# Attention on one core: TensorE's instruction order planned over all sixteen passes at once, row maxima turned six units into the next pass, outputs copied out of PSUM one or two tiles later

## The reference

```python
scores = jnp.einsum('bhqd,bhkd->bhqk', q, k) * scale
causal = jnp.tril(jnp.ones((t, t), dtype=bool))
scores = jnp.where(causal[None, None], scores, -jnp.inf)
att = jax.nn.softmax(scores, axis=-1)
y = jnp.einsum('bhqk,bhkd->bhqd', att, v)
```

## Time and profile before

| what | us |
|---|---|
| median of three runs (lowest 3022.57, highest 3024.21) | 3024.12 |
| the profiled execution, its own time | 3017.77 |
| its span, first to last instruction | 3015.9 |
| attention: the maxima of pass 0 alone | 366.9 to 467.4 |
| attention: first scores to the last copy | 467.4 to 2120.4 |
| busy over the span: PE, DVE, ACT, POOL | 2606.6, 1957.8, 1479.5, 775.3 |

### The profile page before, as it was taken

The page is one execution under the profiler, slowest core; times in us unless marked ns, Lnnn a source line. Parts: engine busy times, 40 slices in busy tenths (PEclk is TensorE's granted clock), DMA queues, the critical chain, the costliest instruction groups (busy, mean ns, idle before and its releaser), DMA issues. The chain is left out here.

```text
span 3015.9 us, 46437 instructions
## 1 busy us (share of the span) xinstructions
PE 2606.6 (86%) x16224; PEld 1332.4 (44%) x16225; DVE 1957.8 (65%) x2820; ACT 1479.5 (49%) x2726; POOL 775.3 (26%) x836
## 2 busy tenths in 40 slices
PE   6988189999999999989999999998666689898880
PEld 6545023333333333333333333332455577787770
DVE  4666297778777877867877787770364333465564
ACT  0555105777767777757777777778222211111110
POOL 0344401111110111011011001111348322474554
PEclk7989558999999999999999999999877799999995
DMA  3577871414531551452355134000764422453443
GB/s 109 143 217 206 161 97 57 100 46 100 117 67 58 121 109 53 81 117 68 57 117 103 36 59 69 13 9 16 200 189 161 152 89 90 126 164 117 133 135 121
DMA packets 210668, 315.39 MB, mean 105 GB/s; under 512 B 31312, under 2 KB 154336, under 8 KB 208192
## 3 DMA queue, kind: packets, MB, share of 16 engines
q1 hardware_dynamic: 163984, 206.55, 29.6%
q0 software_dynamic: 28944, 90.60, 10.1%
q10 hardware_dynamic: 17568, 16.00, 1.5%
HBM read 159.05 MB, written 153.22 MB: 104 GB/s over the span
## 5 line engine op out<-in xcount | busy, mean ns | idle before, releaser
L967 DVE TENSOR_REDUCE mxc<-ps 128x2 f32<-128x1024 f32 (+4 forms) x1168 | 1292.4, 1149 | 297.7 <-PE ps L859 148.5
L949 ACT ACTIVATE probs<-ps 128x512 f32<-128x512 f32 (+1 forms) x2240 | 1159.4, 589 | 400.9 <-PE ps L885 387.3
L859 PE MATMUL ps<-ks,qs 96*128 96x512 bf16 (+3 forms) x2560 | 701.4, 364 | 89.7 <-DMA vs<-v_ones 67.1
L885 PE MATMUL ps<-qs,ks 99*128 99x512 bf16 (+3 forms) x2560 | 686.9, 349 | 10.2 <-ACT probs L949 8.1
L899 PE MATMUL ps<-probs,vs 128*32 128x512 f32 (+3 forms) x5120 | 596.6, 543 | 13.2 <-POOL probs L822 13.2
L859 PEld LDWEIGHTS ps<-ks,qs 96*128 96x128 bf16 x2560 | 205.2, 99 | 554.4 <-issue 202.4
L822 POOL TENSOR_SCALAR_AFFINE_SELECT probs<-probs 128x512 f32<-128x512 f32 x256 | 162.9, 647 | 960.2 <-ACT probs L949 959.0
L885 PEld LDWEIGHTS ps<-qs,ks 99*128 99x128 bf16 x2560 | 221.3, 97 | 421.9 <-ACT probs L949 301.7
L1527 ACT ACTIVATE hid_t<-ps 128x512 f32<-128x512 f32 x125 | 74.7, 597 | 495.2 <-PE ps L1500 451.6
L1500 PE MATMUL ps<-x_t,w_at 128*128 128x128 f32 x2000 | 264.7, 288 | 48.4 <-DVE w_at L1548 41.6
L1500 PEld LDWEIGHTS ps<-x_t,w_at 128*128 128x128 f32 x2000 | 244.2, 199 | 90.3 <-issue 64.9
(11 more groups left out here) (171 smaller groups left out, 1910.4 us busy)
## 6 DMA issues: line engine op xcount, KB each, us to landing
ks<-k_parts SPq DMA_DIRECT2D x96, 256.0 KB, 15.3
qs<-q_parts SPq DMA_DIRECT2D x96, 256.0 KB, 16.2
v_ones<-vout SPq DMA_DIRECT2D x64, 256.0 KB, 4.5
vs<-v_ones SPq DMA_DIRECT2D x16, 1024.0 KB, 26.0
attn_t<-o_sb SPq DMA_DIRECT2D x64, 256.0 KB, 4.7
xs<-slot_x SPq DMA_DIRECT2D x128, 128.0 KB
slot_y<-ys ACTq DMA_DIRECT2D x122, 128.0 KB, 1.7
slot_x<-zero POOLq DMA_DIRECT2D x24, 640.0 KB, 6.2
```

The costliest lines, as they stand in the source:

```text
L859: ins = pe.matmul(o[:, h, :], qs[0:SROWS, r, h0 + h, i * P:(i + 1) * P], ks[0:SROWS, r, h0 + h, 512 * c:512 * c + w], start=first, stop=no ...
L885: ins = pe.matmul(o[:, h, :], ks[0:SROWS + MROWS, r, h0 + h, j * P:(j + 1) * P], qs[0:SROWS + MROWS, r, h0 + h, J * QJ + lo:(J + 1) * QJ], ...
L949: act.activation(probs[:, (NKT * r + m) % NPB, h0:h0 + nh, 0:QJ - lo], st_view(r, s), ACT.Exp, scale=DH ** -0.5).then_inc(exp_done, 1)
L967: dve.tensor_reduce(mxc[:, h0:h0 + nh, i, c], red_view(u, g0), AX_X, ALU.max).then_inc(red_done, 1)
```

## The change

The list is made once for all 16 passes by a new class `Course`, with other costs, with a model of GpSimd's masks and split, of VectorE, and of the landing of the maxima's rows. It chooses among the instructions that its model holds ready by which of ScalarE and VectorE would run dry first. How far VectorE's units may run ahead of the scores is a share of a pass (`RUN_AHEAD`). The turn of pass n stands after unit 5 of pass n+1 on all engines (`LATER`), also at the start, where ten units stood behind the turn. ScalarE copies a block out after the exps of the second tile that follows it (`OUT_LAG`), also over the border of two passes. TensorE waits for the maxima's rows at the first scores of each pass and for a pass's loads at its unit 0. GpSimd's and SP's code is unchanged. The diff, cut to its core:

```diff
--- before.py
+++ after.py
@@ -585,58 +585,129 @@
-def plan(tiles, sets, of_tile, last, diag, groups, nst, npb, cut, turn_at, qj):
-
-    MM, EXP, RED, MASK, COPY, CROSS, BACK, SWITCH = 1 / 2400, 0.81e-3, 1.04e-3, 0.834, 0.58, 0.2, 0.13, 0.14
...
-        if g < len(groups):
-            free = red_end[-2] + BACK if g > 1 else 0.0
-            if (g < near and share[g] <= (done[s - 1] if s else 0) / done[start[cut] - 1] + 0.01) or (
-                    g >= near and s >= start[turn_at]):
-                now.append((free, "group", g))
...
-        at, kind, x = next((c for c in now if c[0] <= pe + 0.1), None) or min(now)
...
+class Course:
+
+
+    MM, MUL, MASK, ENTER, LEAVE, LATE, HOP = 1 / 2400, 0.0045, 0.0565, 0.09, 0.147, 0.1, 0.2
+    TURN_PE, TURN_DVE, ROWS, SPLIT, AFFINE, OUT, LAST_MAX, LOAD = 0.29, 0.5, 3.0, 1.6, 0.65, 0.58, 0.45, 30.0
+    RUN_AHEAD, PREFER_DVE = 0.16, 0.3
...
+        while s < ns * nit or v < nv * nit or g < len(self.stream):
...
+                n, u = self.stream[g]
+                at = red_end[g - self.nred] + hop if g >= self.nred else 0.0
+                if u == turn_unit:
+                    ok = n in parts
+                    at = max(at, parts.get(n, 0.0) + hop)
+                else:
+                    ok = g <= first_turn or s >= ns * nit or dve_at[g] <= (
+                        1 + s // ns + share[s % ns] + self.RUN_AHEAD) * per_group
+                if u == 0 and n >= 3:
+                    ok = ok and n in loaded
+                    at = max(at, loaded.get(n, 0.0))
+                if ok:
+                    now.append((at, "unit", n, u))
+            if s < ns * nit:
+                n, x = divmod(s, ns)
+                tile = n * nv + sets[x][0]
+                before = tile - self.out_lag - 1
+                ok = n in rows_in and v > tile - self.npb and not (before >= 0 and before % nv in self.last and v <= before)
+                if ok and not (n + 1 < nit and x == self.of_tile[self.first_masked][-1] and n + 1 not in neg):
+                    at = exp_end[s - self.nst] + hop if s >= self.nst else 0.0
+                    now.append((max(at, rows_in[n]) if x == 0 else at, "scores", n, x))
...
+                if v in ready and (j > 0 or out < 0 or out in out_end):
+                    now.append((max(ready[v], out_end[out] if j == 0 and out >= 0 else 0.0) + hop, "values", n, m))
+            base = pe + (self.LEAVE if kind == "values" else 0.0)
+            urge = {"unit": dve - pe, "scores": act - pe - self.PREFER_DVE, "values": 1e9}
+            free = [c for c in now if c[0] <= base]
+            at, what, n, x = min(free, key=lambda c: urge[c[1]]) if free else min(now)
...
+                if h0 == 0:
+                    before = tile - self.out_lag - 1
+                    if before >= 0 and before % nv in self.last:
+                        act = max(act, values_end[before] + hop) + self.OUT
+                        out_end[before // nv * self.nj + tiles[before % nv][0]] = act
+                    if tile >= self.npb:
+                        act = max(act, values_end[tile - self.npb] + hop)
+                act = max(act, pe + hop) + self.exp(nh * w)
+                exp_end.append(act)
...
+                    if m in self.diag:
+                        pool = max(pool, act + hop) + self.AFFINE
+                        ready[tile] = pool
...
-        AHEAD = 10
-        NRING = NGRP + 1
-        CUT, TURN_AT = 34, 37
-        entry_of = [(1, u) for u in range(AHEAD, NGRP)] + [(1, TURN)] + [(2, u) for u in range(AHEAD)]
...
+        LATER = 6
+        OUT_LAG = 2
+        NRED = 2
+        assert NSET * R % NST == 0 and NKT * R % NPB == 0
+
+        STREAM = []
+        for n in range(NIT):
+            STREAM += [(n, u) for u in range(LATER)] + [(n - 1, TURN)] * (n > 0) + [(n, u) for u in range(LATER, NGRP)]
+        STREAM.append((NIT - 1, TURN))
+        unit_at = {x: at for at, x in enumerate(STREAM)}
+        ORDER = Course(KT, SETS, of_tile, LAST, DIAG, [GROUPS[u][3:] + (GROUPS[u][1] == GROUPS[u][0] // 4,) for u in range(NGRP)],
+                       STREAM, NST, NPB, NRED, OUT_LAG, QJ, DIAG[-KPJ]).order(NIT)
...
-        RECIP_AT = 30
+        RECIP_AT = 40
...
-                def group(r, u, at, g0):
+                def group(n, u, at):
-                    diag = c == i // 4
-                    if not isinstance(at, int) or at >= 2:
-                        pe.wait_ge(red_done, at - 1)
+                    r, o, diag = n % R, red_view(u, at), c == i // 4
+                    if u == 0:
+                        pe.wait_ge(ld[r], LD * (n // R + 1))
+                    if at >= NRED:
+                        pe.wait_ge(red_done, at - NRED + 1)
...
+                    if s == 0:
+                        pe.wait_ge(m_ld, M_LD * n + M_LD + 1)
                     pe.wait_ge(exp_done, NSET * n + s + 1)
...
-                def entry(n, r, q):
-
-                    ahead, u = entry_of[q]
-                    at = NRING * n + RING0 + q
-                    if u == TURN:
-                        turn(n + 1, at, q)
+                pe.wait_ge(pool_init, R)
+                for kind, n, x in ORDER:
+                    if kind == "scores":
+                        scores(n, n % R, x)
+                    elif kind == "values":
+                        values(n, n % R, x)
+                    elif x == TURN:
+                        turn(n, unit_at[n, x])
                     else:
-                        group((r + ahead) % R, u, at, q)
-
-                def body(n, r, i, more=True, far_more=True):
-                    pe.wait_ge(m_ld, M_LD * n + M_LD + 1)
-                    for kind, x in ORDER:
-                        if kind == "scores":
-                            scores(n, r, x)
-                        elif kind == "values":
-                            values(n, r, x)
-                        elif more and (far_more or entry_of[x][0] == 1):
-                            if entry_of[x] == (2, 0):
-                                pe.wait_ge(ld[(r + 2) % R], LD * i + LD * ((r + 2) // R + 1))
-                            entry(n, r, x)
-
-                pe.wait_ge(ld[0], LD)
-                for u in range(NGRP):
-                    group(0, u, u, u)
-                pe.wait_ge(ld[1], LD)
-                turn(0, NGRP, NGRP)
-                for u in range(AHEAD):
-                    group(1, u, NRING + u, u)
-                pe.wait_ge(pool_init, R)
-                for n in range(NIT):
-                    body(n, n % R, n // R, n + 1 < NIT, n + 2 < NIT)
+                        group(n, x, unit_at[n, x])
...
-                        if m - 1 in LAST.values():
-                            output(n, KT[m - 1][0])
-                    output(n, NJ - 1)
-
-                for n in range(NIT):
-                    body(n, n % R)
+                def exps(n, r, m):
+                    lo = KT[m][2]
+                    act.wait_ge(pv_done, NKT * n + m + 1)
...
+                for tile in range(NIT * NKT + OUT_LAG + 1):
+                    n, m = divmod(tile - OUT_LAG - 1, NKT)
+                    if n >= 0 and m in LAST.values():
+                        output(n, KT[m][0])
+                    if tile < NIT * NKT:
+                        exps(tile // NKT, tile // NKT % R, tile % NKT)
...
-                def body(n, far_more=True):
-                    for q, (ahead, u) in entries(far_more):
-                        if q == RECIP_AT and n > 0:
-                            reciprocals(n - 1)
-                        at = NRING * n + RING0 + q
-                        if u == TURN:
-                            turn(n + 1, at, q)
-                        else:
-                            group(u, at, q)
-                            if u == NGRP - 1:
-                                maxima(n + 1, at + 1)
-
-                for u in range(NGRP):
-                    group(u, u, u)
-                maxima(0, NGRP)
-                turn(0, NGRP, NGRP)
-                for u in range(AHEAD):
-                    group(u, NRING + u, u)
-                for n in range(NIT - 1):
-                    body(n, n + 2 < NIT)
+                for at, (n, u) in enumerate(STREAM):
+                    if u == RECIP_AT and n > 1:
+                        reciprocals(n - 2)
+                    if u == TURN:
+                        turn(n, at)
+                    else:
+                        group(u, at)
+                        if u == NGRP - 1:
+                            maxima(n, at + 1)
```

156 lines of the change are left out of this document (86 added, 70 removed).

## The result

The changed kernel takes 3059.70 us (median of four runs, 3053.58 to 3061.55); the kernel before, run beside it, 3024.16 (3022.57 to 3030.34). The ratio is 1.0115, with a 95% interval of 1.0100 to 1.0131: 35.5 us slower, where 21 us less were forecast. The profiled execution took 3060.03 us, with a span of 3058.1. Of all executions in this document one, of the kernel with the turn at once further down, ran at a granted clock of 0.80, where that kernel's others have 0.92, and took 3415.92 us; it counts in that kernel's median and not in its ratio.

The account below looks back on a forecast made before the run. TensorE bounds a pass, busy 102.63 of 103.54 us. Start 2.0, borders 16.8, passes 4 and 8 -1.0, last pass 3.5 sum to 21.3 off 3017.8; plus 6.3 for the median gives 3002.8 us, range 2991 to 3018.

Parts of the forecast that it names:

- The denominators' wait: Nine passes with fills: VectorE wants the denominators' read earlier, TensorE waits 0 to 2.2 us in each; 0.3 taken.
- each us by which they start later behind the fills is paid back in part: Loads after the block 3 copy: started later they take less time, 30.6 us without fills instead of 37.7.
- my latest bound: Denominators' read in passes with fills: lands at most 2.9 us later, at 716.6, a TensorE wait of 2.2.
- The fixed capacity shared by two streams: DMA engines, loads beside fills: if they only shared capacity, the end of both would not move; wait 0.
- My rival with the full wait: Read lands 2.9 later in nine passes, TensorE waits 2.2 in each: 3021 us; chance 0.17 for about halfway or more.
- the likeliest range of 2996 to 3010: Whole kernel, median time: the forecast case's own range around 3002.8 us, chance 0.55.
- The start: Before the first scores: they come at about 464.8 instead of 467.42; gain 2.0 us, bounds 0 and 3.
- Passes 4 and 8: GpSimd's stuck fill stays: pass 4 loses 2 us, pass 8 gains 1; net loss 1, between loss 4 and gain 5.
- The floor of a pass, and the border: Border of two passes, 14 times: waiting there goes, a pass lasts 101.9 to 102.0 us, a gain of 1.6.
- the slower rival that I priced: Block copies, later by four exps, hold the next block's values at 60 places: 3030 to 3039 us; chance 0.05.
- The last pass: Last pass, with the end of pass 14: 3.5 of 5.4 us gained, bounds 0 and 5.4; full tiles stay at 2.46.
- my 1.6: Gain in us forecast for each border of two passes, before 0.2 off for small waits.

Follow-up runs that it names:

- the kernel with the turn at once: Changed kernel with the turn right behind its maxima (`LATER = 0` instead of 6) and fills behind the mask of tile 23: 3011.90 us, ratio 0.9960.

## Why the prediction was wrong

It failed at one term, and by a smaller sum at another. Both are landings of transfers.

**The denominators' wait: the failed step.** The prediction named the mechanism, and the profile after has it word for word. What failed is "I expect the read 0.7 later, at the earliest bound, and 2.9 at the latest", with "each us by which they start later behind the fills is paid back in part", and from it "I take 0.3". Measured from tile 39's scores at the border of passes 1 and 2, at 681.77 in the changed kernel and 670.67 before:

- The copy ends at 7.4, as forecast (688.55 + 0.58 - 681.77).
- The loads start at 9.2, where 8.3 would have been 2.9 later than before. The missing 0.9 is one row: SP's issue of the reciprocals' store between them took 1.36, and the row of the kernel before below has 0.45. I did not count it. In passes 12 and 13, without fills, the loads do start at 8.2.
- From the first load to the end of the read it takes 38.5 us, not less than the 37.7 of the earlier trace rows. The read's packets end at 47.7, against 43.1 before: 4.6 later, and 1.7 past my latest bound. VectorE takes it up at 48.2.
- VectorE asks at 42.7 (forecast 42.8; before, it came at 47.4). So it waits 5.45, and TensorE 3.97, where I had 0 to 2.2 for TensorE.

```profile
675.55 0.45 SPq L772 DMA_DIRECT2D rden<-rec  x1
```

Why the loads did not get shorter shows in the queues of the DMA engines (packets, MB, share; q0 carries the fills, q1 SP's transfers). Three stretches of the kernel before (676 to 682 beside fresh fills, 682 to 690 beside fills, 698 to 706 alone), and then two of the changed kernel (691 to 697 and 700 to 716):

```profile
q1 hardware_dynamic: 268, 0.29, 15.6%
...
q0 software_dynamic: 294, 1.08, 56.8%
q1 hardware_dynamic: 299, 0.95, 47.9%
...
q1 hardware_dynamic: 280, 0.93, 102.2%
```

```profile
q0 software_dynamic: 445, 1.65, 87.1%
q1 hardware_dynamic: 223, 0.28, 13.7%
...
q1 hardware_dynamic: 555, 1.82, 103.2%
```

In 682 to 690 of the kernel before, beside fills, the loads move 0.95 MB in 8 us; in 698 to 706, alone, 0.93 MB: the fills cost them nothing there, so having them drained earlier gives nothing back. In the changed kernel the loads move 0.28 MB in the 6 us from 691, while the fills move 1.65, and later, alone, 1.82 MB in 16 us, which is the old rate of 0.11 MB a us. I took the length of a pass without fills (30.6) as proof that later is shorter. It only says that the first few us beside fresh fills are slow: 0.29 MB in the first 6 us before, and 0.28 in the changed kernel, so the loads still met them. With the fills in mid-pass they take 32 to 35 us. The fixed capacity shared by two streams, which I weighed beside the round-robin by packet of the Trainium skill ("DMA: Bandwidth & Descriptors", Queues, rings and completion order), would have left their end where it was; it moved by 4.6, so that reading is out. The 294 and 299 packets of the two queues in 682 to 690 agree with such turns; the 445 and 223 in 691 to 697 do not.

**The price of a stall.** My rival with the full wait put TensorE's loss at 2.2 a pass and came to 3021. The gap was 3.97 and the half clock behind it cost 2.6 more, which no term of mine contained, though the earlier trace rows had it: pass 8 waited 9.31 and was 11.8 us longer than its neighbours. Nine passes at 2.2 would have cost 20 us. Eight at 6.6 and one at 2.7 cost 55. With this term gone (reciprocals at unit 60) the kernel takes 3006.88 us, inside the likeliest range of 2996 to 3010; there the 8.3 us lost at the start and the unforeseen 3 of pass 8 stand against each other in part.

**The start.** Forecast 464.8, measured 473.1. From the end of the negated maxima to the copied rows it took 6.9 us (455.13 to 462.06), where I had 5.6. The larger miss is "landed 2.4 later": the earlier trace rows was taken from a pass where the fills come after the rows, and moving the turn six units later put it behind GpSimd's first fills. From the copied rows to the first scores it took 11.0 us instead of 4.4, and 3.9 with those fills moved, where the first scores stand at 463.9 and 464.8.

**Passes 4 and 8.** TensorE waits 4.69 in pass 4 (forecast about 5), and the pass is 1.2 longer than before (forecast 2 us lost). Pass 8 waits 7.41 and is 4.2 shorter (forecast a gain of 1); mis-sized, on the good side. The mechanism was right: in both kernels and both passes the stuck fill starts 0.62 us after the fill ahead of it has landed (906.85 and 907.47 in pass 4, 1348.17 and 1348.79 in pass 8). The prediction did not see that these two would be spared the wait for the read: TensorE's stall at their start gives the read time. In pass 4 its reciprocal starts at 949.38 with no wait.

**The floor of a pass, and the border.** Right: 101.9 to 102.0 forecast, 102.03 to 102.04 measured wherever nothing is late (the terms of its sum, as written, give 101.5, not 101.6). No copy held the values, and the masks of ordinary passes were on time, so the slower rival that I priced did not come. The one that did, I had put on the other side of zero.

**The last pass.** 3.5 forecast, 1.5 measured (85.1 to 83.6), within its bounds. The full tiles, forecast to stay at 2.46, take 2.40; ScalarE's idle time in each is 0.33 instead of 0.39:

```profile
2113.00 2.06 ACT L998 ACTIVATE probs<-ps 128x512 f32<-128x512 f32 x4 [0.33 <-PE ps L956]
...
2115.40 2.06 ACT L998 ACTIVATE probs<-ps 128x512 f32<-128x512 f32 x4 [0.33 <-PE ps L956]
```

**Pass 0.** It is 1 us longer than before, not 1.6 shorter, and 106.7 with the fills moved. The clock explains it. From the first scores TensorE runs at 1.2 GHz for 4.4 us before, 7.6 changed and 9.2 with the fills moved; the rows of the first two:

```profile
467.42:471.80 4.38, 4.38 (x15) 1.67 (x14) 3.31 (x4) 3.58 (x6) 0.00 (x0) 0.50 0.88 302
...
473.09:480.70 7.61, 7.29 (x30) 3.78 (x31) 3.15 (x4) 5.09 (x9) 1.23 (x2) 0.50 0.00 2
```

Half of that time is lost. Less that half, pass 0 takes 102.8 before and 102.1 in both others, where an ordinary pass of the new order takes 102.0. So 0.7 was gained, and my 1.6 left the half clock out.

**Open.** Why the loads beside fresh fills get only a seventh of the traffic, and later half of it, was not tested, nor why the store's issue took 1.36.

## What to carry to other kernels

When a reorder leaves only tenths of a us of slack at a wait, price the wait with what follows it: here a stop of 4 us cost 6.6, in eight of sixteen passes, while the gain was 1.5. A small read that is issued behind bulk loads of its own queue is as late as they are, so look for every consumer whose due time the reorder pulls forward, and move the read ahead or the consumer back before counting the gain. And take a transfer's landing time from a row with the same traffic ahead of it: 2.4 us became 7.9 because the fills had gone first.

## What the runs showed that I had not expected

- The DMA engines show busy shares near 1.0 both at 115 GB/s (loads alone) and at 322 (with fills): the share does not tell how much room is left.
- TensorE's stops of 3.25, 3.97, 4.69, 7.41 and 9.31 us were followed by a loss to the 1.2 GHz level of 1.6, 2.6, 2.9, 1.7 and 2.5 us (the length of the pass, less the stop and an ordinary pass). It did not grow with the stop. In the old order with the reciprocals earlier, four passes lost 1.5 to 3.0 us of waiting and no clock.
- GpSimd's stuck fill (4.85 and 7.57 us) sticks in passes 4 and 8 at both places where the fills were put: moved by half a pass it waits 4.85 and 7.86. It is the 27th and the 53rd fill in all fourteen traces, and it starts 0.62 us after the one ahead has landed.
- The kernel before takes 2983.7 us on one chip and 3024 on two others, and 37 of the 40 us lie in the stage behind the attention (896 against 859 us, the second read from the old order with the fills in mid-pass).
